# Six re-orderings in a one-core attention and sparse FFN kernel: seeds, magnitudes, weight loads, splits and row steps

## The reference, cut to what matters

```python
xn = _layernorm(x)
x = x + _L0_attn_ref(xn, qkv, o_proj, gamma, beta) + _L0_ffn_ref(xn, w_gate, w_up, w_down)

# _L0_attn_ref(x = xn)
x_norm = layernorm(x) * gamma + beta
q, k, v = x_norm @ qkv[:, :512], x_norm @ qkv[:, 512:1024], x_norm @ qkv[:, 1024:]
attn = softmax(causal(q @ k.T / sqrt(512)))
out = (attn @ v) @ o_proj + x

# _L0_ffn_ref(x = xn), w_gate and w_up 512 x 2048, w_down 2048 x 512
h = silu(x @ w_gate) * (x @ w_up)
h_sparse = h where it is among the 2 largest |h| of its group of 4, else 0
return h_sparse @ w_down
```

## Time and profile before

| | |
|---|---|
| time, median of 3 runs | 825.08 us (823.86 to 826.26) |
| profiled execution, its own time | 825.98 us |
| its span, first to last instruction | 823.9 us |
| outside the span | 2.1 us |
| mean granted TensorE clock | 0.993 of full speed |
| PE busy | 810.0 us, 98% of the span |
| DVE busy | 580.8 us, 70% |
| ACT busy | 304.4 us, 37% |
| DMA, mean | 143 GB/s |

### The profile page before, as it was taken

How to read it: one execution, slowest core, us unless ns; L and a number is a source line. 1 busy time by engine, 2 the same in 40 slices (tenths; PEclk the granted TensorE clock), 3 DMA queues, 4 the chain that set the end, 5 groups by cost and what they waited for, 6 DMA issues and landing times.

```text
span 823.9 us, 9546 instructions
## 1 busy us (share of the span) xinstructions
PE 810.0 (98%) x3643; PEld 664.1 (81%) x3643; DVE 580.8 (70%) x998; ACT 304.4 (37%) x500; POOL 13.9 (2%) x33
## 2 busy tenths in 40 slices
PE   9999999999999999999999999997999999999998
PEld 6778888888888888888878878876888888888886
DVE  6857777446532448769999799798558559559886
ACT  6423223112211225563635535363225235235341
POOL 2010101000000000000000000000000000000000
PEclk9999999999999999999999999998999999999999
DMA  9421442040201027566463461584646342352002
GB/s 322 163 107 61 141 140 77 26 129 27 76 24 54 27 94 289 193 245 240 179 229 104 179 230 52 206 324 185 229 179 221 162 184 76 149 200 77 6 0 103
DMA packets 30284, 117.55 MB, mean 143 GB/s; under 512 B 2928, under 2 KB 2976, under 8 KB 27808
## 3 DMA queue, kind: packets, MB, share of 16 engines
q1 hardware_dynamic: 26064, 109.35, 35.8%
q10 hardware_dynamic: 4176, 7.60, 2.8%
HBM read 74.98 MB, written 41.97 MB: 142 GB/s over the span
## 4 chain that ended last, share of the span: by engine, by line
PE 76%; DVE 5%; ACT 5%; DMA 4%; issue 2%; SPq 0%; DVEq 0%; ACTq 0%
PE bank L668 9%; PE bank L514 9%; PE bank L516 9%; PE bank L515 9%; PE bank L669 9%; PE bank L670 9%; PE bank L742 6%; PE bank L744 6%; PE bank L743 6%; PE bank L571 4%; ACT mag L890 2%; DMA w_operands<-wset 2%; PE bank L555 2%; DMA dw_raw<-L_ffn_w_down 2%; DVE wset L1023 1%
## 5 line engine op out<-in xcount | busy, mean ns | idle before, releaser
L668 PE MATMUL bank<-X_hi,wset 128*128 128x512 f32 x448 | 177.0, 395 | 5.4 <-ACT g_sum L886 4.2
L669 PE MATMUL bank<-X_lo,wset 128*128 128x512 f32 x448 | 175.4, 391 | 0.0
L670 PE MATMUL bank<-X_hi,wset 128*128 128x512 f32 x448 | 175.3, 391 | 0.0
L668 PEld LDWEIGHTS bank<-X_hi,wset 128*128 128x128 f32 x448 | 84.8, 189 | 28.6 <-ACT bank L886 5.2
L670 PEld LDWEIGHTS bank<-X_hi,wset 128*128 128x128 f32 x448 | 84.7, 189 | 18.0
L669 PEld LDWEIGHTS bank<-X_lo,wset 128*128 128x128 f32 x448 | 84.8, 189 | 17.1
L742 PE MATMUL bank<-dw,hs_hi 128*128 128x512 f32 x224 | 87.6, 391 | 0.4
L744 PE MATMUL bank<-dw,hs_lo 128*128 128x512 f32 x224 | 87.2, 389 | 0.0
L743 PE MATMUL bank<-dw,hs_hi 128*128 128x512 f32 x224 | 87.2, 389 | 0.0
L1239 DVE TENSOR_TENSOR acc<-bank,acc 128x512 f32<-128x512 f32 x60 | 40.8, 688 | 45.5 <-PE bank L744 45.5
L514 PE MATMUL bank<-xT_hi,zg_hi 128*128 128x512 f32 (+3 forms) x160 | 59.0, 369 | 0.0
(11 more groups left out here) (175 smaller groups left out, 1370.4 us busy)
## 6 DMA issues: line engine op xcount, KB each, us to landing
w_operands<-wset SPq DMA_DIRECT2D x8, 3584.0 KB, 11.9
wset<-w_operands SPq DMA_DIRECT2D x8, 3584.0 KB, 11.5
wsum<-w_units SPq DMA_DIRECT2D x28, 256.0 KB, 3.9
dw_raw<-L_ffn_w_down SPq DMA_DIRECT2D x14, 512.0 KB, 5.5
xw<-L_attn_x SPq DMA_DIRECT2D x4, 1024.0 KB, 9.7
xt_raw<-x_t SPq DMA_DIRECT2D x8, 512.0 KB, 7.5
xn_t<-xt_raw SPq DMA_DIRECT2D x8, 512.0 KB, 5.2
acc<-resid SPq DMA_DIRECT2D x2, 2048.0 KB, 9.9
```

Of the source, the lines that this page charges most:

```text
L668: pe.matmul(dst[:], u[:, 0, :], x_hi, start=(first and kt == 0), stop=False, skip_group_check=True)
L669: pe.matmul(dst[:], u[:, 0, :], x_lo, start=False, stop=False, skip_group_check=True)
L670: last = pe.matmul(dst[:], u[:, 1, :], x_hi, start=False, stop=(kt == 1), skip_group_check=True)
```

## The change: what it does

1. Start: 9 matmuls on the zeroed tile, where there were 8.
2. Chunk 0's row steps: the order `xh_pre[k]`, `xh[k]`, `z_round[k]` becomes `xh_pre[0]`, then for each k `xh_pre[k+1]`, `xh[k]`, `z_round[k]`. DVE thus scales tile k+1 while ACT casts tile k.
3. A new step `row_copy` holds the copy of the turned statistics. For chunk 1 it stands ahead of `v[0][1]`, so that DVE does it before it splits that tile; for chunks 2 and 3 the order stays as it was. PE's order is unchanged.
4. Chunk 1: `xh_pre[1][0]` moves from row tile 0 to row tile 1, and the next tiles move with it; the last two tiles, 2 and 3, both are scaled and split after the head of row tile 3.
5. `X_order(1)`: T4 is split ahead of T3, where T3 was ahead of T4.
6. SP, step 7: `load_down(3)` with its wait for `down(5)` stands ahead of `load_made(9)`.
7. ACT, steps 3 to 7 and 9 to 14: two magnitudes, gate seed, two magnitudes, up seed, where there were four magnitudes and two seeds.
8. DVE, steps 3 to 6: the four `operands_lo` and the first adds stand as lo 0, add 0, lo 1, lo 2, add 1, lo 3, add 2, where they stood as lo 0, lo 1, add 0, lo 2, lo 3, add 1, add 2.

```diff
-    steps += [step for k in range(KT) for step in (xh_pre[0][k], xh[0][k], z_round[0][k])]
+    steps.append(xh_pre[0][0])
+    steps += [step for k in range(KT) for step in (*xh_pre[0][k + 1:k + 2], xh[0][k], z_round[0][k])]
...
-              ("scores", 0, 0), exp[0], ("x_turn", 0, 1), x_scale[1], v[0][1], row_turn[1], row_store[1], row_spread[1]]
+              ("scores", 0, 0), exp[0], ("x_turn", 0, 1), x_scale[1], row_copy[1], v[0][1], row_turn[1], row_store[1], row_spread[1]]
...
-    between = {3: [z_round[1][1], xh_pre[1][3], xh[1][2], z_round[1][2], xh[1][3], z_round[1][3], *z[1], xn[1][0], v[1][0], xn[1][1],
-                   xn_store[1], xt_load[2]],
+    between = {3: [xh_pre[1][2], xh[1][2], z_round[1][1], z_round[1][2], xh_pre[1][3], xh[1][3], z_round[1][3], *z[1], xn[1][0],
+                   v[1][0], xn[1][1], xn_store[1], xt_load[2]],
...
-    beside = {0: [v[0][2], xh_pre[1][0]],
-              1: [xh_pre[1][1], v[0][3], xh[1][0]],
-              2: [xh_pre[1][2], xh[1][1]],
+    beside = {0: [v[0][2]],
+              1: [xh_pre[1][0], v[0][3], xh[1][0]],
+              2: [xh_pre[1][1], xh[1][1]],
...
-            return X_ORDER if p == 0 else (B11, B21, T2, T1, B22, T3, T4)
+            return X_ORDER if p == 0 else (B11, B21, T2, T1, B22, T4, T3)
...
+                if n == NQ - 1:
+                    sp.wait_ge(down_full, TC * (d + 1))
+                    load_down((d + 1) // 2)
                 if n + 2 < N_Q and n != NQ - 2:
...
-                if d >= 0 and d % 2 == 1 and d + 1 < ND:
+                if d >= 0 and d % 2 == 1 and d + 1 < ND and n != NQ - 1:
...
-            for _ in range(8):
+            for _ in range(9):
...
-                    if i >= 0 and n < N_Q - 1:
-                        magnitudes(i)
-                    seeds(n)
+                    picks = i >= 0 and n < N_Q - 1
+                    if picks:
+                        magnitudes(i, (0, 1))
+                    gate_seed(n)
+                    if picks:
+                        magnitudes(i, (2, 3))
+                    up_seed(n)
...
-                elif kind == "row_turn":
-                    no = turn_no[kind, n]
+                elif kind == "row_copy":
+                    no = turn_no["row_turn", n]
...
                     operands_lo(n + 1, 0)
+                    add_down(i, 0)
                     operands_lo(n + 1, 1)
-                    add_down(i, 0)
                     operands_lo(n + 1, 2)
+                    add_down(i, 1)
                     operands_lo(n + 1, 3)
-                    add_down(i, 1)
                     add_down(i, 2)
```

More of the change, by code:

```diff
@@ L59, in attention_ffn @@
     xh_pre, xh, z, z_round, v = ([fills(kind, c) for c in range(NCH)] for kind in ("xh_pre", "xh", "z", "z_round", "v"))
-    x_stats, x_rstd, x_scale, row_turn, xw_load, row_store, row_spread, xt_load, xn_store = (
-        [(kind, c, 0) for c in range(NCH)] for kind in ("x_stats", "x_rstd", "x_scale", "row_turn", "xw_load", "row_store",
+    x_stats, x_rstd, x_scale, row_turn, row_copy, xw_load, row_store, row_spread, xt_load, xn_store = (
+        [(kind, c, 0) for c in range(NCH)] for kind in ("x_stats", "x_rstd", "x_scale", "row_turn", "row_copy", "xw_load", "row_store",
                                                         "row_spread", "xt_load", "xn_store"))
@@ L81, in attention_ffn @@
                11: [*z_round[3], *xn[3], xn_store[3], *z[3], v[3][0]]}
-    beside = {0: [v[0][2], xh_pre[1][0]],
-              1: [xh_pre[1][1], v[0][3], xh[1][0]],
-              2: [xh_pre[1][2], xh[1][1]],
+    beside = {0: [v[0][2]],
+              1: [xh_pre[1][0], v[0][3], xh[1][0]],
+              2: [xh_pre[1][1], xh[1][1]],
               3: [*stat[2], x_stats[2], x_rstd[2], v[1][1]],
-              4: [x_scale[2], v[1][2], row_turn[2], row_store[2], *xn[0], row_spread[2], xn_store[0]],
+              4: [x_scale[2], v[1][2], row_turn[2], row_copy[2], row_store[2], *xn[0], row_spread[2], xn_store[0]],
               5: [v[1][3], xh_pre[2][0], xh[2][0]],
@@ L89, in attention_ffn @@
               7: [x_scale[3], xn[2][0]],
-              8: [v[2][1], row_turn[3], row_store[3], row_spread[3]],
+              8: [v[2][1], row_turn[3], row_copy[3], row_store[3], row_spread[3]],
               9: [v[2][2]],
@@ L901, in last_silu @@
                 nc.scalar.activation(g_sum[1][:], g_sum[1][:], ACT.Silu).then_inc(silu_ready, 1)
-            def seeds(n):
-                gate_seed(n)
-                up_seed(n)
             def gate_seed(n):
```

## The result

The changed kernel takes 810.34 us (median of 4 runs, 809.83 to 811.26), the kernel before 824.52 in the same comparison (823.86 to 826.26): a ratio of 0.983 (0.981 to 0.985), 14.2 us. The profiled execution took 810.05 us, with a span of 808.1 and a mean granted clock of 1.000; against the profiled one of before the span is 15.8 us shorter. That one had more half clock than any of the 25 later executions of before: these were granted 0.995 to 0.998 on average, where it had 0.993.

A forecast was written before the change was run, and what follows sets the result against it. PE was taken as the bound, busy for 98% of the span, with gains in its late starts. Terms +0.2 -1.4 -1.3 -3.4 -1.5 -7.2 = -14.6 from 825.1 gave 810.5 us; range 807.0 to 814.5.

The forecast's parts named there:

- Step 8: FFN step 8: T4 before T3 and earlier down weights remove waits and slow matmuls, less a late DVE sum; -7.2 us.
- Rival C: Step 8 mended only in part: down weights land at 560 or DVE is 1.5 behind; 814 us, chance 0.10.
- D: Set 9, read behind the down weights, comes late for step 9; slower than before, 832 us if at 600; chance 0.02.
- E: Step 8: T3 last does nothing, as something else holds T4's cast; PE waits 0.9 as before, 811.4 us; chance 0.03.
- Seeds: ACT, eleven steps: the gate seed between the magnitudes removes a late PE start of 0.31 us each; -3.4 us.
- Rival B: The later comparison eats the seeds' gain: a bank late by 0.3 in each of eleven steps, 813.9 us; chance 0.09.
- Chunk 0: Row steps two tiles deep: PE's 1.20 us wait at 41.02 for z's first lo part goes; -1.4 us.
- The new stops at chunk 1's tiles 2 and 3: PE waits 1.1 to 1.2 us for tile 2 and 1.1 us more for tile 3; +2.3 us.
- Chunk 1 with row_copy: Row tiles near 61: earlier rows remove a stop and slow matmuls (-3.6 us), new stops cost 2.3; -1.3 us.
- Adds: DVE, steps 3 to 6: earlier adds remove four late PE starts of 0.38 us before tile 2; -1.5 us.
- The ninth warm matmul: Kernel start: one more matmul costs 0.45 us at most, an earlier clock rise may give back more; +0.2 us.
- Rival A: The new stops at chunk 1's tiles 2 and 3 pull the clock down; 812.2 us, or 814 with two slow stretches; chance 0.14.

The follow-up runs named there:

- experiment 2: The changed kernel with ACT's four magnitudes ahead of both seeds again; 813.53 us.
- experiment 7: The changed kernel with chunk 0's row steps one tile deep again; 812.31 us.
- experiment 6: The changed kernel with chunk 1's placement and the copy of the turned rows both as before; 810.53 us.
- experiment 5: The changed kernel with chunk 1's tiles placed as before, the early copy of the turned rows kept; 811.08 us.
- experiment 11: The changed kernel with down weights ahead of the store in steps 3 and 5, chunk 1's tile 2 scaled beside row tile 2, tile 3 before tile 2's split; 807.09 us.
- experiment 3: The changed kernel with DVE's old order of weight splits and adds in steps 3 to 6; 811.00 us.
- experiment 4: The changed kernel with the down weights issued ahead of the weight set's store in steps 3 and 5 too; 809.21 us.
- experiment 1: The changed kernel with SP's order in step 7 put back, the down weights behind set 9; 817.63 us.
- experiment 10: The changed kernel with down weights ahead of the store in steps 3 and 5, and chunk 1's tile 2 scaled in row tile 2; 807.69 us.

## Why the prediction was right, and where it was not

**The total** was forecast at 810.5 and came to 810.34, a change of 14.6 against 14.2. The fit is closer than the terms are. Four of these were about right and two were too large, by some 2 us together (chunk 1 and the adds); chunk 0 and step 8 gave more than forecast, and the sum starts from 825.1, 0.6 above the median of the comparison. That these cancel is luck. The prediction also read its terms from the profiled execution, the one with the most half clock, and took them from the median: a granted clock of 0.998, as in 11 of the 25 later executions of before, leaves 3.3 us at half clock, where the profiled one had 3.5 and 6.9.

**Step 8** (-7.2): right, -7.43 in the traces, and 7.2 and 1.1 when its two edits are undone one at a time. The two overlap, since what T3 delays is caught in part by the wait for the down weights. The queue was read rightly: the load went out at 543.16, at the end of down(5), its halves landed at 548.53 and 549.77, behind the store's end at 545.93 (it did not overtake), and ACT, ready at 551.83, never waited for it. The late DVE sum was put at 0.6 and is 0.29. Rival C did not come; nor did D, as set 9 landed at 559.14 and PE wanted it in step 9, from 573.37 on; nor E, as PE's wait for the gate seed is gone.

**Seeds** (-3.4): right in mechanism and size; undone, it costs 3.1 in the medians and 0.34 to 0.37 a step, 3.8 in all, in the trace. Up's seed kept its margin. Rival B did not come: no bank is late in the eleven steps, and the stop in step 8 is there without this edit too (experiment 2).

**Chunk 0** (-1.4): right. v[0][0] follows its forerunner without a wait; undone, it costs 1.9, for where DVE sets the pace an early rise of the clock gives nothing: it only turns up as one more stop, at 37.01 (experiment 7). Stops that the trace of before doesn't show can stand just behind the ones it shows.

**The new stops at chunk 1's tiles 2 and 3:** right in place, mechanism and size: 1.15 and 0.94, forecast 1.1 to 1.2 and 1.1.

**Chunk 1 with row_copy** (-1.3): the step that failed. The removal was credited with 3.6, the old stop (2.1) and the slow matmuls behind it (1.5). Against the profile of before the two traces do bear it out (1.60 gained from v[0][0] to step 0), but experiment 6, with the old placement and the old copy, has nearly all of that gain: there the removal is worth 2.40 and the new stops cost 2.34, and the medians say 0.1. What was wrong is to take the stop of 2.15 and the half clock behind it, read from one execution, for what stays when only this part is left out: with the rest of the change in place the stop is 0.97 and the clock never falls. The rows took 6.0 us through DRAM there and 7.2 before; whether chance or another part of the change made that difference isn't shown. And the 1.5 of slow matmuls was priced as if PE could have run at full pace there: at full clock, in experiments 5 and 6, two stops of 0.5 and 0.7 stand in their place. Also, `row_copy` was to bring the rows 1.1 sooner; in experiment 5 the store took 3.1 us instead of 1.4, and they came no sooner.
That the placement moves stops rather than removing them is shown by experiments 5 and 6; that none is needed, by experiment 11.

**Adds** (-1.5): the term was right by itself, four late starts of 0.4 are gone, but what the edit sets off was not counted. The last lo part of DVE comes later, the store of the set with it, and in step 4 the store is then so near ahead of the down weights that these stop PE in four of nine traces, which gives 0.7 back (experiments 3 and 4). Undone, the edit costs 0.6. In the list of what stands behind each moved instruction, SP's store, which waits for it, was missing.

**The ninth warm matmul** (+0.2): no difference that can be told; the forecast is neither borne out nor refuted.

**Rival A**, the clock, did not come: in none of the fourteen traces did PE fall to half clock behind a stop of 0.3 to 1.4 us. It did behind 2.15 (before), and at the stops of 4.35 (before) and 5.85 (experiment 1). So the doubt in the prediction about the Trainium skill's "TensorE: Matmul & The Clock Gate", section "HAM oscillation", stays as it was: new stops were harmless, as the page has it, but the stop of 2.15 us in the trace of before was followed by half clock, which by the page it should not have been. There the measurement decides; it is one stop in one trace.

## What to carry to other kernels

When PE is 98% busy, look for late starts, not for costly groups, and take a second trace before pricing a stop that hangs on a transfer, since one execution's stop, and the slow matmuls behind it, need not be there in the next. Two edits that bear on one place can't be added: what one delays, the wait for the other hides (T3 and the down weights in step 8). For each instruction that moves on an engine, list the transfers that wait for it as well, and what stands behind these in the same queue. A load that is needed soon goes ahead of a store that nobody waits for.

## What the runs showed of the hardware

- The first half (512 KB) of the down weights of step 4 landed 10.2 to 11.3 us after its issue when it was issued 2.8 us behind a 3.5 MB store on the same queue (nine traces), 10.0 and 10.1 when 3.8 us behind it (experiment 3 and before), and 5.1 when ahead of it (experiments 4, 10 and 11).
- The 8 KB store of the turned rows took 1.4 us in five traces and 2.4 to 3.1 in nine, for the same instructions; the 1 MB read behind it took 4.2 to 5.8. Store and read together took 6.0 to 7.7: such a round trip through DRAM can't be planned to a microsecond.
- The clock first rose 4.3 to 7.0 us after the first instruction in thirteen traces, and at 10.0 in the fourteenth (experiment 11), whose first product also started 0.6 us or more later than any other's. That run took 3.0 us more than the median of the other three.
- A matmul that starts 0.2 us late at full clock costs 0.3: the one behind it is 0.1 late as well.
